# Two of four gathered groups turned by VectorE blocks and transfers inside SBUF instead of by TensorE

## The chip, the cores and the metric

The kernel runs on one core of a Trainium2 chip. The metric is the device time of one execution in microseconds (us). A kernel is run several times and the median is compared; besides, one execution is recorded by the hardware profiler, and every duration below comes from that one.

## The reference, cut to what matters

`x` is 64 batches of 32 rows by 256 features. Each batch goes through an attention block with two feed-forward nets, and then through three adapters whose weights are picked by the batch's role:

```
q, k, v = x @ Wq, x @ Wk, x @ Wv
attn_out = softmax(q k^T * scale) v @ Wp + bp
cms_out  = gelu(attn_out @ cW1 + cb1) @ cW2 + cb2 + onehot(code)
modifier = gelu(concat(attn_out, cms_out) @ mW1 + mb1) @ mW2 + mb2
x = clip(x + cms_out + modifier, 0, 1)
for layer in 3 adapters:        # weights and biases of the batch's role
    x = layernorm(x + gelu(x @ W_down + b_down) @ W_up + b_up) * gamma + beta
```

## The kernel before

Batches are sorted by role, and the 2048 rows are cut into four groups of 512 rows (`NG = 4`; the code numbers them 0 to 3, so the third and the fourth are group 2 and group 3). The feed-forward work on them runs in five waves (the last group is split in two), and the adapters of the windows (128 rows each) of one wave run in between the matmuls of the next. Everything is written out by hand, one instruction stream for each engine, with semaphores between them. A wave is a list of steps: `("H", n)` computes hidden block n on TensorE (PE), gelu and the high part of the result on ScalarE (ACT), the low part `h_lo` on VectorE (DVE); `("D", n)` multiplies that block into the result; `C` and `F` close the two nets. A matrix in float32 is split in a high and a low part and multiplied in three passes (`mm3`, lines 332 to 334).

The attention of a group is cut in parts that are hung onto such steps by the table `ATTENTION`. The rows of a group are gathered from HBM by an indirect transfer of GpSimd (POOL) into `xr`, 128 partitions of rows by 256 features, four tiles (`GT = 4`). But the matmuls want features in the partitions: `xT`. So for groups 2 and 3 part `X` (wave 0 after `H10`, wave 1 after `H5`) lets PE turn the eight 128x128 pieces into two PSUM banks (line 1365), ACT copies them to `xT` (819), ACT makes the high part `parts_hi` (822) and DVE the low part `parts_lo` (1042). Part `Y`, two steps later, multiplies them with a folded weight whose low part `fold_lo` is made by DVE (1252) just before. Then come scores `S`, softmax `P`, the weighted sum `Z` (which reads `xr` again) and the projection `A`, `B`. Groups 0 and 1 have an attention of their own at the start, in halves.

The order of the work around the change, on the two engines that issue transfers:

- POOL: gathers of groups 0 and 1; then it waits for the adapters' biases, sums two of them (`brow`, line 752); then it gathers group 2 once the `Z` of group 0 is through; and group 3 at the end of wave 0, after the `Z` of group 2, since both use the buffers of the first attention.
- SP (the sync engine's queue): weights in chunks, then some 30 transfers that pack the adapters' weights into a table in HBM (`packed_w`, `packed_rows`, lines 561 to 590; the last six, line 590, wait for DVE's `dbias`), then a wait for all of these (598, 599), then the loads of the adapters' weights window by window (606 to 614). Later layers of some windows are turned by DVE in 32x32 blocks (`block_rows`, line 1143) and moved into place by four transfers inside SBUF (`move_blocks`, line 643).

Of the kernel before, what the change touches and what calls it, by code (L numbers as in the profile page):

```python
# [12 lines left out]
P = 128  # L13
B, T, V = 64, 32, 256
H = 4 * V
# [43 lines left out]
def build(nc, x, codes, roles, Wq, Wk, Wv, Wp, bp, cW1, cb1, cW2, cb2, mW1, mb1, mW2, mb2, adapters, out):  # L59
# [3 lines left out]
    with ExitStack() as ctx:  # L63
# [3 lines left out]
        def sem(name):  # L67
            return ctx.enter_context(nc.semaphore(name))
# [175 lines left out]

        def high(cols):
            return c_hi[:, cols] if cols.stop <= MW1 else m_hi[:, cols.start - MW1:cols.stop - MW1]
# [43 lines left out]
        xT_turned = sem("xT_turned")  # L290
# [95 lines left out]
        ATTENTION = {0: {("H", 10): ("X", 2), ("H", 12): ("Y", 2), ("H", 13): ("S", 2), ("H", 14): ("P", 2),  # L386
# [147 lines left out]
        def _(sp):  # L534
# [46 lines left out]
            for layer in range(LAYERS - 1):  # L581
# [3 lines left out]
                         allow_slow_non_contiguous=True).then_inc(weights_packed, 16)  # L585
            sp.wait_ge(down_bias_ready, 1)
# [104 lines left out]
            for n, w, layer in items:  # L691
                if n and items[n - 1][1:] in moves:
                    move_blocks(*items[n - 1][1:])
                ahead = (w, layer) == (MIXED[0], 0)
                if ahead:
                    window_rows(*items[n - 1][1:])
                window_weights(w, layer)
                if 0 < n <= len(items) - len(ending) and not ahead:
                    window_rows(*items[n - 1][1:])
# [12 lines left out]
        def _(pool):  # L712
# [23 lines left out]

            def gather(g):
                for t in range(GT):
                    pool.indirect_dma_start(out=attention(g).xr[:, t, :], out_offset=None, in_=x_rows,  # L739
                                            in_offset=bass.IndirectOffsetOnAxis(ap=row_idx[:, g * GT + t:g * GT + t + 1],  # L740
                                                                                axis=0))\
                        .then_inc(x_in[g] if g >= AHEAD else half_in[2 * g + t // (GT // 2)], 16)
# [7 lines left out]
            gather(1)  # L750
            pool.wait_ge(adapter_in, 16 * ADAPTER_DMAS)
            pool.tensor_tensor(brow[:, 0, :], brow[:, 0, :], brow[:, 1, :], ALU.add).then_inc(brow_summed, 1)
            pool.wait_ge(more_consts, 3)
            pool.wait_ge(z_done, VB)
            gather(2)
# [29 lines left out]
        def _(act):  # L785
# [28 lines left out]
            def attention_part(stage_name, g):  # L814
                a = attention(g)
                if stage_name == "X":
                    act.wait_ge(xT_turned, g - AHEAD + 1)
                    for vb in range(VB):
                        act.activation(xT[:, vb, bass.ts(g, GR)], a.banks[vb][:, :], ACT.Copy).then_inc(xT_ready, 1)
                    for vb in range(VB):  # L820
                        act.wait_ge(xT_ready, 2 * VB * (g - AHEAD) + vb + 1)
                        act.activation(parts_hi[:, vb, :], xT[:, vb, bass.ts(g, GR)], ACT.Copy).then_inc(xT_ready, 1)
# [135 lines left out]
        def _(dve):  # L958
# [78 lines left out]
            def attention_part(stage_name, g):  # L1037
                a = attention(g)
                if stage_name == "X":
                    for vb in range(VB):  # L1040
                        dve.wait_ge(xT_ready, 2 * VB * (g - AHEAD) + VB + vb + 1)
                        dve.tensor_tensor(parts_lo[:, vb, :], xT[:, vb, bass.ts(g, GR)], parts_hi[:, vb, :].bitcast(F32),
                                          ALU.subtract).then_inc(xT_lo_ready, 1)
                if stage_name == "Z" and g >= AHEAD:
                    for vb in range(VB):
                        dve.wait_ge(z_ready, VB * g + vb + 1)
                        dve.tensor_tensor(parts_lo[:, vb, :], a.banks[vb][:, :], parts_hi[:, vb, :].bitcast(F32),
                                          ALU.subtract).then_inc(z_lo_ready, 1)
# [163 lines left out]
            for g, step in steps:  # L1212
# [28 lines left out]
                if g == 1 and step == ("H", 0):  # L1241
                    dve.wait_ge(eps_ready, 2 * SLOTS)
                if g == NM - 1 and step == ("H", HB + 2):
                    last_sum(last[0])
# [34 lines left out]
        def _(pe):  # L1279
# [76 lines left out]
            def attention_part(stage_name, g):  # L1356
                a, first = attention(g), g * GR
                if stage_name == "X":
                    pe.wait_ge(x_in[g], 16 * GT)
                    if g > 1:  # L1360
                        pe.wait_ge(at_hi_ready, VB * (1 if g == 2 else 3))
                        pe.wait_ge(at_lo_ready, VB * (1 if g == 2 else 3))
                    for vb in range(VB):
                        for i in range(GT):
                            ins = pe.transpose(a.banks[vb][:, i * P:(i + 1) * P], a.xr[:, i, vb * P:(vb + 1) * P],
                                               ident[:, :])
                    ins.then_inc(xT_turned, 1)
                if stage_name == "Y":
                    pe.wait_ge(xT_ready, 2 * VB * (g - AHEAD + 1))
# [20 lines left out]
                if stage_name == "Z":  # L1390
                    pe.wait_ge(pd_ready, g + 1)
                    for vb in range(VB):
                        for i in range(GT):
                            ins = pe.matmul(a.banks[vb][:, i * P:(i + 1) * P], a.xr[:, i, vb * P:(vb + 1) * P],  # L1394
                                            a.pd[:, i, :], start=True, stop=True)
                        ins.then_inc(z_done, 1)
# [327 lines left out]
```

## Time and profile before

| | |
|---|---|
| median of 3 runs | 353.15 us (353.07 to 354.5) |
| time of the profiled execution | 353.24 us |
| its span in the trace | 351.4 us |
| PE busy | 340.3 us, 97% of the span |
| DVE, ACT, POOL busy | 59%, 48%, 18% |
| granted TensorE clock | full (2.4 GHz) in every slice |
| DMA queue of SP | 33910 packets, 45.6% of 16 engines |

The span is what the trace covers; the 1.8 us between it and the time lie before the first and after the last instruction. Times "at 70.14" below are microseconds from the span's start. A matmul's own duration in the trace overlaps the next one, so what it costs is read from the distance between starts.

### The profile page before, as it was taken

To read this page: it belongs to the slowest core of one execution; us is meant where nothing else is said; L and a number is where in the kernel's file an instruction comes from. 1 tells how busy PE (TensorE), PEld (TensorE's weight loads), DVE (VectorE), ACT (ScalarE), POOL (GpSimd) and SP (SyncE) were. 2 spreads that over 40 slices of the span, in tenths; PEclk is the share of its full clock that TensorE was granted. 3 is DMA by queue.
4 is the path that set the end of the run, shared out by engine and by line. 5 is a ranking of instruction groups with operands and counts; after the bars stand their busy time and mean duration, and the time that the engine had idled before them with its cause. 6 is when DMAs were issued, how large, how long until landed. Compare 5 with 4: busy or idle time off the path is not lost.

```text
span 351.4 us, 6683 instructions
## 1 busy us (share of the span) xinstructions
PE 340.3 (97%) x2247; PEld 283.2 (81%) x2247; DVE 206.5 (59%) x493; ACT 167.3 (48%) x331; POOL 61.9 (18%) x96
## 2 busy tenths in 40 slices
PE   6899999999999999999999999999999999999994
PEld 6677687787778888788877777877899999999962
DVE  6057367350462885577464665463689777454584
ACT  3465686464543553644154455353355454634421
POOL 2710040000040110011420110013321135100221
PEclk9999999999999999999999999999999999999999
DMA  6574699558210314233176898203957432288001
GB/s 219 174 236 153 175 128 146 39 118 176 67 60 0 87 41 116 76 97 115 48 238 164 253 292 253 62 30 109 204 149 207 144 125 87 71 274 339 25 2 45
DMA packets 35704, 46.93 MB, mean 134 GB/s; under 512 B 9852, under 2 KB 20406, under 8 KB 35670
## 3 DMA queue, kind: packets, MB, share of 16 engines
q1 hardware_dynamic: 33910, 42.51, 45.6%
q0 software_dynamic: 1392, 3.80, 3.8%
q8 instruction: 18, 0.29, 0.4%
q10 hardware_dynamic: 368, 0.20, 0.2%
q14 instruction: 16, 0.13, 0.1%
HBM read 43.60 MB, written 4.48 MB: 137 GB/s over the span
## 4 chain that ended last, share of the span: by engine, by line
PE 84%; DVE 6%; ACT 3%; POOL 3%; issue 3%; DMA 1%; POOLq 0%; DVEq 0%
PE bank L332 12%; PE bank L334 11%; PE bank L333 11%; PE bank L1490 8%; PE bank L1495 8%; PE bank L1491 8%; PE bank L1537 4%; PE bank L1513 3%; PE bank L1394 2%; PE bank L1352 2%; PE bank L1412 2%; ACT h_full L847 1%; ACT h_hi L851 1%; PE bank L1568 1%; PE bank L1616 1%
## 5 line engine op out<-in xcount | busy, mean ns | idle before, releaser
L847 ACT ACTIVATE h_full<-bank,bias 128x512 f32<-128x512 f32 (+1 forms) x80 | 48.2, 603 | 111.2 <-PE bank L334 101.7
L1079 DVE TENSOR_TENSOR h_lo<-h_full,h_hi 128x512 fp32r<-128x512 f32 (+1 forms) x80 | 46.8, 585 | 60.4 <-ACT h_hi L851 57.3
L767 POOL TENSOR_TENSOR rstd<-moments,minus_half 128x1 f32<-128x1 f32 x39 | 24.9, 638 | 167.1 <-DVE moments L1152 166.9
L851 ACT ACTIVATE h_hi<-h_full 128x512 fp32r<-128x512 f32 (+1 forms) x80 | 43.7, 546 | 2.5
L1137 DVE TENSOR_TENSOR window_y<-bank,window_x 128x256 f32<-128x256 f32 x39 | 16.5, 423 | 36.9 <-PE bank L1513 25.5
L1490 PE MATMUL bank<-h_hi,m_hi 128*128 128x512 f32 (+1 forms) x80 | 30.2, 387 | 0.2
L1490 PE MATMUL bank<-h_hi,c_hi 128*128 128x512 f32 (+1 forms) x80 | 30.1, 385 | 0.2
L332 PE MATMUL bank<-at_hi,c_hi 128*128 128x512 f32 (+1 forms) x80 | 29.3, 367 | 0.0
L332 PE MATMUL bank<-at_hi,m_hi 128*128 128x512 f32 (+1 forms) x80 | 28.7, 359 | 0.0
L334 PE MATMUL bank<-at_lo,c_hi 128*128 128x512 f32 (+1 forms) x80 | 27.9, 348 | 0.0
L333 PE MATMUL bank<-at_hi,c_lo 128*128 128x512 f32 (+1 forms) x80 | 27.8, 347 | 0.0
L334 PE MATMUL bank<-at_lo,m_hi 128*128 128x512 f32 (+1 forms) x80 | 27.8, 347 | 0.0
L333 PE MATMUL bank<-at_hi,m_lo 128*128 128x512 f32 (+1 forms) x80 | 27.7, 347 | 0.0
L1491 PE MATMUL bank<-h_hi,m_lo 128*128 128x512 f32 (+1 forms) x80 | 27.2, 349 | 0.0
L1491 PE MATMUL bank<-h_hi,c_lo 128*128 128x512 f32 (+1 forms) x80 | 27.1, 348 | 0.0
L739 POOL DMA_INDIRECT xr<-in_x,row_idx x16 | 15.4, 963 | 58.8 <-PE bank L1394 49.2
L332 PE MATMUL bank<-cms_hi,m_hi 128*128 128x512 f32 (+1 forms) x70 | 24.3, 346 | 0.0
L333 PE MATMUL bank<-cms_hi,m_lo 128*128 128x512 f32 (+1 forms) x70 | 24.3, 346 | 0.0
L334 PE MATMUL bank<-cms_lo,m_hi 128*128 128x512 f32 (+1 forms) x70 | 24.2, 346 | 0.0
L1128 DVE SCALAR_TENSOR_TENSOR window_x<-window_y,rstd,adapter_rows 128x256 f32<-128x256 f32 x39 | 18.7, 480 | 5.6 <-POOL rstd L767 4.2
L1495 PE MATMUL bank<-h_lo,c_hi 128*128 128x512 f32 (+1 forms) x80 | 21.6, 351 | 0.1
L1495 PE MATMUL bank<-h_lo,m_hi 128*128 128x512 f32 (+1 forms) x80 | 21.4, 348 | 0.0
(238 smaller groups left out, 727.9 us busy)
## 6 DMA issues: line engine op xcount, KB each, us to landing
adapter_w<-packed_w SPq DMA_DIRECT2D x44, 256.5 KB, 3.6
adapter_rows<-packed_rows SPq DMA_DIRECT2D x36, 256.0 KB, 5.5
stage<-in_L_cond_mW SPq DMA_DIRECT2D x6, 512.0 KB, 5.3
mixed_w<-packed_w SPq DMA_DIRECT2D x8, 256.5 KB, 4.6
stage<-in_L_cond_cW SPq DMA_DIRECT2D x4, 512.0 KB, 6.8
last_w<-packed_w SPq DMA_DIRECT2D x2, 769.5 KB, 6.3
up_bias<-in_L_cond_b_up SPq DMA_DIRECT2D x12, 128.0 KB, 4.2
adapter_rows<-packed_rows SPq DMA_DIRECT2D x24, 64.0 KB
```

The lines of the kernel that those rows point to most:

```text
L332: pe.matmul(o, w_hi_ap, r_hi_ap, start=first, stop=False)
L333: pe.matmul(o, w_lo_ap, r_hi_ap, start=False, stop=False)
L334: return pe.matmul(o, w_hi_ap, r_lo_ap, start=False, stop=last)
L767: pool.tensor_tensor(slot.rstd[:, :], slot.moments[:, 1:2], minus_half[:, :], ALU.pow)\
L847: act.activation(h_full[:, n % 2, rows], bank[n % 2][:, rows], ACT.Gelu, bias=bias[:, b:b + 1])\
L851: act.activation(h_hi[:, n % 2, rows], h_full[:, n % 2, rows], ACT.Copy).then_inc(h_hi_ready, 1)
L1079: dve.tensor_tensor(h_lo[:, n % 2, rows], h_full[:, n % 2, rows], h_hi[:, n % 2, rows].bitcast(F32), ALU.subtract).then_inc(h_lo_ready, 1)
L1128: dve.scalar_tensor_tensor(slot.x[:, :], slot.y[:, :], slot.rstd[:, :], slot.rows[:, 1, :], ALU.mult, ALU.add).then_inc(slot.x_ready, 1)
L1137: dve.tensor_tensor(slot.y[:, :], bank[6][:, 0:V], slot.x[:, :], ALU.add).then_inc(emptied[6], 1)
L1490: pe.matmul(results[ob][:, rows], high(cols), h_hi[:, n % 2, rows], start=(j == 0), stop=False)
L1491: pe.matmul(results[ob][:, rows], low(cols), h_hi[:, n % 2, rows], start=False, stop=False)
L1495: ins = pe.matmul(results[ob][:, rows], high(cols), h_lo[:, n % 2, rows], start=False, stop=(j == HB - 1))
```

## The change

For groups 2 and 3 part `X` leaves PE. DVE transposes each row tile in 32x32 blocks (four new parts `T0` to `T3`), and SP moves each block row into `xT` by four transfers inside SBUF, 16 for a group (`spread_x`). ACT only makes the high part. Group 2's gather stands ahead of the bias sum on POOL. Group 3's `xr` is still in use when its blocks are wanted, so its rows are gathered twice: first into the columns of `xT` that group 3 will own (`x_raw`), for the blocks, and later into `xr` as before, for `Z`. The blocks of group 2 stand in `yz`, those of group 3 in the `window_y` tiles of the four adapter slots, and DVE waits before wave 1 uses these.

```diff
+        def x_blocks(g, t):
+            return (attention(g).yz[:, :, :].rearrange("p k m -> p (k m)")[:, bass.ts(t, V)] if g == AHEAD
+                    else slots[t].y[:, :])
+
+        def x_raw(t):
+            return xT[:, t // 2, bass.ds((NG - 1) * GR + t % 2 * V, V)]
...
-        ATTENTION = {0: {("H", 10): ("X", 2), ("H", 12): ("Y", 2), ("H", 13): ("S", 2), ("H", 14): ("P", 2),
+        ATTENTION = {0: {("H", 4): ("T0", 2), ("H", 5): ("T1", 2), ("H", 6): ("T2", 2), ("H", 7): ("T3", 2),
+                         ("D", 10): ("T0", 3), ("D", 11): ("T1", 3), ("D", 12): ("T2", 3), ("D", 13): ("T3", 3),
+                         ("H", 10): ("X", 2), ("H", 12): ("Y", 2), ("H", 13): ("S", 2), ("H", 14): ("P", 2),
...
+            def spread_x(g):
+
+                for t in range(GT):
+                    sp.wait_ge(x_blocked, t + 1 if g == AHEAD else 2 * GT)
+                    for q in range(Q):
+                        sp.dma_start(xT[:, :, bass.ds(g * GR + t * P + q * T, T)],
+                                     x_blocks(g, t)[quarter(q), :].rearrange("p (f m) -> p f m", f=Q)).then_inc(x_spread, 16)
+
+            spread_x(AHEAD)
             sp.wait_ge(down_bias_ready, 1)
...
+                if n == len(WAVES[1]) + 1:
+                    spread_x(AHEAD + 1)
...
+            pool.wait_ge(z_done, VB)
+            gather(2)
             pool.wait_ge(adapter_in, 16 * ADAPTER_DMAS)
             pool.tensor_tensor(brow[:, 0, :], brow[:, 0, :], brow[:, 1, :], ALU.add).then_inc(brow_summed, 1)
             pool.wait_ge(more_consts, 3)
-            pool.wait_ge(z_done, VB)
-            gather(2)
+            pool.wait_ge(down_bias_done, 1)
+            for t in range(GT):
+                gather_rows(NG - 1, t, x_raw(t))
...
                 if stage_name == "X":
-                    act.wait_ge(xT_turned, g - AHEAD + 1)
+                    act.wait_ge(x_spread, 16 * Q * GT * (g - AHEAD + 1))
                     for vb in range(VB):
-                        act.activation(xT[:, vb, bass.ts(g, GR)], a.banks[vb][:, :], ACT.Copy).then_inc(xT_ready, 1)
-                    for vb in range(VB):
-                        act.wait_ge(xT_ready, 2 * VB * (g - AHEAD) + vb + 1)
                         act.activation(parts_hi[:, vb, :], xT[:, vb, bass.ts(g, GR)], ACT.Copy).then_inc(xT_ready, 1)
...
+                if stage_name[0] == "T":
+                    t = int(stage_name[1])
+                    rows = a.xr[:, t, :] if g == AHEAD else x_raw(t)
+                    dve.wait_ge(x_in[g], 16 * GT)
+                    if g == AHEAD:
+                        dve.wait_ge(at_done, VB)
+                    dve.transpose(x_blocks(g, t).rearrange("p (f k r) -> p k f r", f=Q, k=VB),
+                                  rows.rearrange("p (k i f) -> p k f i", k=VB, f=Q)).then_inc(x_blocked, 1)
...
+                if g == 1 and step == ("H", 2):
+                    dve.wait_ge(x_spread, 16 * Q * GT * (NG - AHEAD))
...
-                if stage_name == "X":
-                    pe.wait_ge(x_in[g], 16 * GT)
...
-                    for vb in range(VB):
-                        for i in range(GT):
-                            ins = pe.transpose(a.banks[vb][:, i * P:(i + 1) * P], a.xr[:, i, vb * P:(vb + 1) * P],
-                                               ident[:, :])
-                    ins.then_inc(xT_turned, 1)
```

On PE, in wave 0 between hidden block 10 and result block 9, the rows were these before (the matmuls of the first net's output with the second net's weights, the turns, the next result block):

```order
L333 MATMUL bank<-cms_hi,m_lo 128x512
L334 MATMUL bank<-cms_lo,m_hi 128x512
L1365 MATMUL bank<-ident,xr 128x128 x8
L1490 MATMUL bank<-h_hi,m_hi 128x512
L1491 MATMUL bank<-h_hi,m_lo 128x512
```

and are these now:

```order
L341 MATMUL bank<-cms_hi,m_lo 128x512
L342 MATMUL bank<-cms_lo,m_hi 128x512
L1517 MATMUL bank<-h_hi,m_hi 128x512
L1518 MATMUL bank<-h_hi,m_lo 128x512
```

Only the eight turns are gone; the same holds in wave 1, where they stood behind the small matmuls of an adapter.

On DVE, at steps H6, H7 and C of wave 0, each chunk of weights (`m_lo`) is now followed by a transpose of one row tile of group 2 into `yz`; the last one stands between `dbias` and the sums that close the first net (`cms`):

```order
L1110 TENSOR_TENSOR h_lo<-h_full,h_hi 128x512
L1057 TENSOR_TENSOR m_lo<-stage,m_hi 128x1024
L1073 STREAM_TRANSPOSE yz<-xr 128x2x4x32
L1110 TENSOR_TENSOR h_lo<-h_full,h_hi 128x512
L1057 TENSOR_TENSOR m_lo<-stage,m_hi 128x1024
L1050 TENSOR_TENSOR dbias<-down_rows,bank 128x256
L1073 STREAM_TRANSPOSE yz<-xr 128x2x4x32
L1118 TENSOR_TENSOR cms<-bank,cms_bias 128x512 x2
```

In every one of these steps the transpose is the only row that is new, and the hidden block's low part waits behind it in the next step.

On SP, the first 16 transfers stand between the packing of `b_down` and that of `dbias`, with the loads of the adapters' weights behind them:

```order
L592 DMA packed_rows<-brow 3x256 x2
L594 DMA packed_w<-in_L_cond_b_down 384x1x1
L601 DMA xT<-yz 128x2x32 x16
L609 DMA packed_w<-dbias 128x1x1 x6
L622 TENSOR_LOAD role_table
```

The second 16 stand in the loads of wave 1, behind the weights of window 1's second layer and ahead of the rows of window 0's second layer:

```order
L625 DMA adapter_w<-packed_w 128x513
L601 DMA xT<-window_y 128x2x32 x16
L629 ISA
L629 DMA adapter_rows<-packed_rows 128x512
```

What moved is only what stands behind them in SP's own order.

## Rows read from the trace of the kernel before

**Rows 1.** The page: the chain that ended last, by engine.

```profile
PE 84%; DVE 6%; ACT 3%; POOL 3%; issue 3%; DMA 1%; POOLq 0%; DVEq 0%
```

**Rows 2.** Timeline of PE, wave 0: start us, us, engine line op out<-in.

```profile
69.91 0.39 PE L334 MATMUL bank<-cms_lo,m_hi 128*128 128x512 f32 x1
70.14 1.03 PE L1365 MATMUL bank<-ident,xr 128*128 128x128 f32 x8
70.94 0.48 PE L1490 MATMUL bank<-h_hi,m_hi 128*128 128x512 f32 x1
71.25 0.39 PE L1491 MATMUL bank<-h_hi,m_lo 128*128 128x512 f32 x1
```

**Rows 3.** The chain that ended last, its pieces at both turns: start us, us, what.

```profile
70.31 0.87 PE bank L1365 x8
...
121.39 0.87 PE bank L1365 x8
```

**Rows 4.** Timeline of PE: what DVE's work is wanted for.

```profile
63.85 0.61 PE L1453 MATMUL bank<-cms_lo,m_hi 128*128 128x512 f32 x2
...
79.29 0.47 PE L332 MATMUL bank<-parts_hi,fold_hi 128*128 128x512 f32 x1
```

**Rows 5.** Timeline of DVE, waves 0 and 1.

```profile
52.41 0.69 DVE L1079 TENSOR_TENSOR h_lo<-h_full,h_hi 128x512 fp32r<-128x512 f32 x1 [0.54 <-ACT h_hi L851]
...
59.94 0.41 DVE L1027 TENSOR_TENSOR dbias<-down_rows,bank 128x256 f32<-128x256 f32 x1
60.49 1.29 DVE L1087 TENSOR_TENSOR cms<-bank,cms_bias 128x512 f32<-128x512 f32 x2
61.88 1.29 DVE L1094 TENSOR_TENSOR cms_lo<-cms,cms_hi 128x512 fp32r<-128x512 f32 x2
...
77.93 1.22 DVE L1252 TENSOR_TENSOR fold_lo<-fold,fold_hi 128x1024 fp32r<-128x1024 f32 x1
...
94.30 1.25 DVE L1065 STREAM_TRANSPOSE pd<-expd 32x128 f32<-32x128 f32 x4
...
111.20 0.42 DVE L1163 TENSOR_TENSOR window_x<-bank,up_bias 128x256 f32<-128x256 f32 x1 [2.82 <-PE bank L1560]
...
126.31 0.63 DVE L1143 STREAM_TRANSPOSE block_rows<-window_x 128x256 f32<-128x256 f32 x1
```

**Rows 6.** Timeline of ACT around part X in wave 0.

```profile
71.60 1.07 ACT L819 ACTIVATE xT<-bank 128x512 f32<-128x512 f32 x2
72.56 1.16 ACT L822 ACTIVATE parts_hi<-xT 128x512 fp32r<-128x512 f32 x2
75.33 0.69 ACT L847 ACTIVATE h_full<-bank,bias 128x512 f32<-128x512 f32 x1 [1.62 <-PE bank L334]
```

**Rows 7.** Timeline of SP's queue: start of the issue, us it took.

```profile
51.17 1.74 SPq L578 DMA_DIRECT2D packed_rows<-in_L_cond_ln_w  x1
...
54.50 0.65 SPq L584 DMA_DIRECT2D packed_w<-in_L_cond_b_down  x1
60.38 3.76 SPq L590 DMA_DIRECT2D packed_w<-dbias  x6
...
83.24 1.49 SPq L606 DMA_DIRECT2D adapter_w<-packed_w  x1
...
126.96 2.60 SPq L643 DMA_DIRECT2D window_xT<-block_rows  x4
```

**Rows 8.** The page: issues of `move_blocks`, KB each, us to landing.

```profile
window_xT<-block_rows SPq DMA_DIRECT2D x24, 32.0 KB, 1.9
```

**Rows 9.** DMA in 139.9 to 142.6, `move_blocks` alone: packets, share of 16 engines.

```profile
DMA packets 320, 0.07 MB, mean 27 GB/s; under 512 B 320, under 2 KB 320, under 8 KB 320
...
q1 hardware_dynamic: 320, 0.07, 13.2%
```

**Rows 10.** Waits of SP's queue: us in total, times, longest.

```profile
SPq L598 <- DMA packed_rows<-brow: 4.4, 1, 4.4
```

**Rows 11.** Timeline of POOL: the first of group 2's four gathers.

```profile
43.97 0.97 POOL L739 DMA_INDIRECT xr<-in_x,row_idx  x1 [0.16 <-issue]
```

More of the change, by code:

```diff
@@ L289, in build @@
         half_y_ready = sem("half_y_ready")
-        xT_turned = sem("xT_turned")
+        x_blocked = sem("x_blocked")
+        x_spread = sem("x_spread")
         xT_ready = sem("xT_ready")
@@ L735, in _, with gather_rows @@
             pool.wait_ge(rows_known, 1)
+            def gather_rows(g, t, o):
+                pool.indirect_dma_start(out=o, out_offset=None, in_=x_rows,
+                                        in_offset=bass.IndirectOffsetOnAxis(ap=row_idx[:, g * GT + t:g * GT + t + 1], axis=0))\
+                    .then_inc(x_in[g] if g >= AHEAD else half_in[2 * g + t // (GT // 2)], 16)
             def gather(g):
                 for t in range(GT):
[L739 to L742, printed above, removed]
+                    gather_rows(g, t, attention(g).xr[:, t, :])
             def store(x_tile, w, counter):
@@ L1040, in attention_part @@
                     for vb in range(VB):
-                        dve.wait_ge(xT_ready, 2 * VB * (g - AHEAD) + VB + vb + 1)
+                        dve.wait_ge(xT_ready, VB * (g - AHEAD) + vb + 1)
                         dve.tensor_tensor(parts_lo[:, vb, :], xT[:, vb, bass.ts(g, GR)], parts_hi[:, vb, :].bitcast(F32),
                                           ALU.subtract).then_inc(xT_lo_ready, 1)
+                if stage_name[0] == "T":
[6 more added lines that the diff above has]
+                                  rows.rearrange("p (k i f) -> p k f i", k=VB, f=Q)).then_inc(x_blocked, 1)
                 if stage_name == "Z" and g >= AHEAD:
@@ L1357, in attention_part @@
                 a, first = attention(g), g * GR
-                if stage_name == "X":
-                    pe.wait_ge(x_in[g], 16 * GT)
-                    if g > 1:
-                        pe.wait_ge(at_hi_ready, VB * (1 if g == 2 else 3))
-                        pe.wait_ge(at_lo_ready, VB * (1 if g == 2 else 3))
-                    for vb in range(VB):
-                        for i in range(GT):
-                            ins = pe.transpose(a.banks[vb][:, i * P:(i + 1) * P], a.xr[:, i, vb * P:(vb + 1) * P],
-                                               ident[:, :])
-                    ins.then_inc(xT_turned, 1)
                 if stage_name == "Y":
-                    pe.wait_ge(xT_ready, 2 * VB * (g - AHEAD + 1))
+                    pe.wait_ge(at_hi_ready, VB * (1 if g == AHEAD else g))
+                    pe.wait_ge(at_lo_ready, VB * (1 if g == AHEAD else g))
+                    pe.wait_ge(xT_ready, VB * (g - AHEAD + 1))
                     pe.wait_ge(xT_lo_ready, VB * (g - AHEAD + 1))
@@ L1391, in attention_part @@
                     pe.wait_ge(pd_ready, g + 1)
+                    if g == NG - 1:
+                        pe.wait_ge(x_in[g], 16 * GT * 2)
                     for vb in range(VB):
```

## Prediction

> **What bounds the kernel now.** I read the page first: the chain that ended last is PE for 84% of the span [rows 1], at full clock everywhere, so a microsecond off PE's stream is a microsecond off the time as long as nobody makes PE wait in its place. Then the timeline of PE at the place that the edit touches [rows 2]: the matmul before the turns starts at 69.91, the turns at 70.14, the next matmul at 70.94, with no gap. Then the timelines of the engines that take over the work, DVE, ACT, SP and POOL, each for the two questions that decide the case: how long does the new work take there, and who wants its result when. PE loses no time in this stretch to DVE or ACT before the change, so every new wait would be visible at once.
>
> **What is removed.** Eight turns last from 70.14 to 70.94, 0.80 us [rows 2]. The change of kind of matmul costs on top: the first start after the turns is followed at 0.31 us (70.94 to 71.25), where 69.91 to 70.14 shows 0.23, so 0.08 more, 0.88 in all. The chain puts each set of turns at 0.87 [rows 3]. In wave 1 small float32 matmuls stand ahead of the turns, so the change of kind stays; I take 0.87 there too. Removed from the path: 0.88 + 0.87 = 1.75 us. ACT also loses its two copies of 1.07 us a group [rows 6], which are off the path.
>
> **DVE's new work.** A transpose of a 128x256 tile of this very pattern takes 0.63 us [rows 5], eight of them are 5.0 us. Seven stand in gaps. Group 2's first three come behind chunks of weights, where DVE had 0.54 idle ahead of `h_lo` [rows 5]: each overhangs by about 0.1, and PE uses the `h_lo` over a microsecond later, so nothing. The fourth stands between `dbias`, which ends at 60.35, and `cms`, which started at 60.49 [rows 5]: the transpose ends at 60.98 and all of `cms` and `cms_lo` moves by 0.49. `cms_lo` ended at 61.88 + 1.29 = 63.17 and would end at 63.66; PE wants it at 63.85 [rows 4]. The cover is 0.19, so the edit costs nothing; if each of the four did overhang by 0.1 more, PE would wait about 0.2. That is my lower and upper bound here: 0 to 0.2. Group 3's stand at D10 to D13 of wave 0, the last after the softmax blocks that end at 94.30 + 1.25 = 95.55 [rows 5]; it ends at 96.18, before PE's next need of `h_lo`.
>
> **POOL's order.** Group 2's gather started at 43.97 because it stood behind the bias sum [rows 11]; POOL sat idle ahead of that, so the gather now runs in idle time, the sum is not moved, and the rows are there long before the first transpose at about 51.9. The additional gather of group 3 starts once the down biases are computed (before `dbias` at 59.94 [rows 5]), and its user comes at about 78. Four gathers of 0.97 are issued by about 65; with the longest landing that a row here shows, some 14 us behind the packing (below, [rows 10]), they would be in at 79, a microsecond after DVE's turn and still ahead of the `h_lo` that comes next. No cost.
>
> **The transfers, group 2.** SP is free at 54.50 + 0.65 = 55.15 [rows 7]. Nothing in the trace has 128-byte runs; the nearest are those of `move_blocks`, 256-byte runs from 32 into 128 partitions: four issues in 2.60 us, 0.65 each [rows 7], 1.9 to land [rows 8]. Sixteen are 10.4 us: 55.15 + 10.4 = 65.6, the last tile's blocks (60.98) being there in time; landed at 67.5. Even if SP began only when the last tile is turned, they would land at 60.98 + 10.4 + 1.9 = 73.3. The upper bound of an issue is the 1.74 us that a small packing transfer took while SP's queue was full [rows 7]: 55.15 + 27.8 + 1.9 = 84.9. The other bound is 0.65/2 if issue went by the bytes of a run. I take 0.65: same kind of source and destination, only the runs are half as long. Who waits? ACT's part `X` started at 71.60 and the next `h_full` at 75.33 [rows 6]. The first to hurt is part `Y`: after the rows are in, ACT needs 1.16 for `parts_hi` [rows 6]; from `h_full` at 75.33 to the end of `fold_lo` at 77.93 + 1.22 = 79.15 [rows 5] are 3.82 us in one chain; together 4.98. PE reached `Y` at 79.29 [rows 4] and will reach it at 79.29 - 0.88 = 78.41. So the transfers must be in by 78.41 - 4.98 = 73.4 to cost nothing, and from 74.3 on the first 0.88 are used up. By my value the cover is 73.4 - 67.5 = 5.9 us.
>
> **How much the DMA engines have to do.** Alone, `move_blocks` shows 320 packets in 2.7 us at 13.2% of 16 engines [rows 9]: 0.132 x 16 x 2.7 / 320 = 17.8 ns a packet. A group's transfers are 16 x (256 + 16) = 4352 packets, 272 an engine: 4.8 us by that price, 2.4 if half the bytes are half the time. Either is below the 10.4 of the issue, so SP's issue decides, not the engines. The weights' packing moves behind it: the six `dbias` transfers from 60.38 [rows 7] to 65.6, and the adapters' loads by 5 us. These loads ended at 83.24 + 1.49 = 84.7 [rows 7] and the first window's sum comes at 111.2 [rows 5]: no cost.
>
> **A rule that speaks against it.** The `packed_rows` of the bias sum were issued before 54.50, and SP still waited 4.4 us for them [rows 10] after its last issue at 60.38 + 3.76 = 64.14 [rows 7], so they counted as landed at 68.5, some 14 us after the issue, where a move inside SBUF took 1.9 [rows 8]. The Trainium skill says why in "DMA: Bandwidth & Descriptors", Queues, rings and completion order: a transfer's completion count is written only after every earlier write of the same DMA engine. By that rule, the trace agrees as far as that row goes. As a mechanism of this kernel, from the rows alone: the new transfers stand behind those slow packing writes, so they would count at 68.5, plus their own 4.8 us of engine time, plus 1.9 to land: 75.2, which is 1.8 too late for `Y`. By the free landing (67.5) the sum is -1.75, by this one -1.75 + 1.8 = 0. I hold the free landing for likelier, since group 2's gather no longer runs among the packing [rows 11] and the backlog should end earlier; the other is a rival.
>
> **The transfers, group 3.** They wait for all eight transposes, 96.18 - 0.88 = 95.3, are issued by 105.7 and landed by 107.6. SP has nothing else to do then: its loads are out, and the next waits for window 0. DVE waits for them before wave 1 touches `window_y`, after the row at 111.20 + 0.42 [rows 5], now 110.7. Cover 3.1 us; an issue of more than (110.7 - 95.3 - 1.9)/16 = 0.84 us uses it up.
>
> **Sum.** 353.24 - 1.75 + 0 = 351.5 for the profiled execution, which stands 0.1 above the median: 351.4 for the median. A change of 0.5% (1.77 us) is about what can be told from none, so this gain is right at that edge.
>
> **Rivals.**
> - *The turned rows of group 2 come late*: packing and moves share the queues, and completion waits for the slow writes. For it the wait of 4.4 us [rows 10] and the issue of 1.74 [rows 7]. Against it that the backlog ends earlier without the gather. At the landing of 75.2 it costs 1.8: 353.2; at the bound of 84.9 it would cost 11.5: 362.9. Chance 0.13.
> - *Group 3's transfers stall DVE* (the one on the other side): if 128-byte runs cost more to issue. At 1.1 us each they land at 95.3 + 17.6 + 1.9 = 114.8, DVE is 4.1 late, and if PE follows the time is 351.4 + 4.1 = 355.5; it is slower than before from an issue of (110.7 + 1.75 - 95.3 - 1.9)/16 = 0.95 us, and by over 0.5% from 1.06. For it: twice the runs of `move_blocks`. Against it: each of these was 0.65 whatever else went on. Chance 0.08.
> - *Part of the gain is given back in small waits*: the overhangs on DVE with only 0.19 of cover at `cms`, `fold_lo` ending 0.14 ahead of `Y`, later waits that do not move with PE. Half of the gain: 352.3. Chance 0.17.
>
> **How the numbers follow.** The forecast, all of the gain, has 0.62. Its own spread is small, 350.8 to 351.8, and it lies on the edge of 0.5%, so I split it. Faster by over 0.5%: 0.62 x 0.65 = 0.40, the larger share because ACT's lighter load may add some tenths. Same: 0.62 x 0.35 = 0.22, with 0.17 and the 0.09 of the first rival that stay near 353.2: 0.48. Slower by over 0.5%: the other 0.04 of it and 0.08, 0.12. The range runs from 350.8 to 354.6, which takes in a small wait and a landing up to 3 us late.
>
> **What would show it.** Right: no rows of turns, 0.23 between the matmuls there; the 16 issues near 0.65 each, ACT's `parts_hi` at about 71 with no wait behind a DMA; PE's `Y` near 78.4; DVE's wait at 110.7 not visible. Wrong: an ACT wait named by a DMA into `xT`, `Y` after 79.3, DVE idle ahead of the first `window_y`, SP issues above 0.84 us, or idle time of PE ahead of the matmuls at 63.85.

## The result and the profile after

The changed kernel takes 357.6 us (median of 6 runs, 356.66 to 358.25), the kernel before took 353.56 us beside it (6 runs, 353.05 to 354.5). The ratio is 1.0113, 95% interval 1.01 to 1.0126: slower, outside my range. The profiled execution took 357.25 us, its span is 355.4, 4.0 more than before. Of the kernel before's executions beside e1 to e3, the three with a mean granted clock of 0.992 took 354.2 to 354.4 us, the ten others 353.0 to 353.4.

The page of the changed kernel, the chain that ended last by engine, where [rows 1] stood before.

```profile
PE 81%; DVE 7%; ACT 3%; POOL 3%; issue 3%; another core or an unknown queue 2%; DMA 1%; POOLq 0%; DVEq 0%
```

PE has gone from 84% to 81%, and 2% of the chain stand behind something that the profile can't name. That share is one single piece. The chain in order of time:

```profile
26.25 2.36 DVE c_lo L1057 x2
28.61 6.03 another core or an unknown queue
...
34.66 0.30 DVE row_max L1084
```

`row_max` is the first step of group 1's softmax, ahead of wave 0: nothing of this is near the turns. The timeline of POOL shows what is new at 28.6, the early gather of group 2:

```profile
28.75 0.95 POOL L759 DMA_INDIRECT xr<-in_x,row_idx  x1 [9.98 <-PE bank L1421]
30.00 0.94 POOL L759 DMA_INDIRECT xr<-in_x,row_idx  x1 [0.30 <-issue]
...
32.50 0.95 POOL L759 DMA_INDIRECT xr<-in_x,row_idx  x1 [0.30 <-issue]
```

The timeline of PE in the kernel before, at group 1's scores (64 matmuls of 32 columns), the projection, and, behind Z, the first matmul of wave 0:

```profile
27.48 0.76 PE L1387 MATMUL bank<-xT,yz 128*32 128x32 f32 x64
28.18 3.70 PE L1412 MATMUL bank<-yz,fold 128*128 128x512 f32 x8
...
33.65 0.47 PE L332 MATMUL bank<-at_hi,c_hi 128*128 128x512 f32 x1
```

The same of the changed kernel, up to wave 0's first matmul at 39.63:

```profile
28.41 0.60 PE L1412 MATMUL bank<-xT,yz 128*32 128x32 f32 x45
29.32 0.27 PE L1412 MATMUL bank<-xT,yz 128*32 128x32 f32 x6 [0.31 <-issue]
30.07 0.28 PE L1412 MATMUL bank<-xT,yz 128*32 128x32 f32 x6 [0.48 <-issue]
30.83 0.28 PE L1412 MATMUL bank<-xT,yz 128*32 128x32 f32 x5 [0.48 <-issue]
31.59 0.24 PE L1412 MATMUL bank<-xT,yz 128*32 128x32 f32 x2 [0.48 <-issue]
31.76 5.40 PE L1439 MATMUL bank<-yz,fold 128*128 128x512 f32 x8
37.82 2.05 PE L1421 MATMUL bank<-pd,xr 128*128 128x128 f32 x16 [0.66 <-DVE pd L1096]
39.63 0.48 PE L340 MATMUL bank<-at_hi,c_hi 128*128 128x512 f32 x1
```

Read it from the top. The two traces are already 0.93 us apart when the scores start (28.41 and 27.48), and this is not the change's doing (e2 below, the same code up to there, starts them at 27.56). The windows (us of the stretch, then the busy share with the number of instructions for PE, PEld, DVE, ACT and POOL, then granted clock, DMA share, GB/s) show it at 16, first in the changed kernel, then in the one before:

```profile
16.00:17.00 1.00, 1.00 (x5) 0.91 (x4) 0.00 (x0) 0.37 (x1) 0.69 (x2) 0.50 0.36 110
```

```profile
16.00:17.00 1.00, 1.00 (x8) 0.90 (x7) 0.00 (x0) 0.70 (x2) 0.69 (x2) 1.00 0.31 73
```

The changed kernel's trace has the granted clock at 0.50, the 1.2 GHz level, from 15 to 19, after three microseconds with PE busy for 0.07, 0.49 and 0.68 (0.82, 0.66 and 0.39 in the kernel before, where it stayed full). The traces of e7 and e11 below have the same fall and start their first scores about a microsecond late; no other has it.

In the changed kernel PE gets through 45 of the 64 matmuls, and then pauses after every five or six, with nothing named that it waits for. The scores take 3.4 us and not 0.76. The first pause comes some 0.25 us after the first gather's issue began. The gathered rows' own packets start only after 31, behind the first three pauses. Then the projection takes 5.40 us for the same eight matmuls. The windows of that stretch show why:

```profile
28.00:29.00 1.00, 1.00 (x50) 0.79 (x49) 0.61 (x1) 0.70 (x2) 0.25 (x1) 1.00 0.52 119
29.00:30.00 1.00, 0.28 (x7) 0.16 (x5) 0.00 (x0) 0.11 (x1) 0.70 (x1) 1.00 0.97 333
30.00:31.00 1.00, 0.44 (x11) 0.34 (x11) 0.00 (x0) 0.00 (x0) 0.94 (x1) 1.00 0.83 259
31.00:32.00 1.00, 0.52 (x8) 0.38 (x4) 0.00 (x0) 0.00 (x0) 0.75 (x1) 1.00 1.00 328
32.00:33.00 1.00, 1.00 (x3) 0.26 (x3) 0.00 (x0) 0.00 (x0) 0.69 (x2) 0.73 0.73 256
33.00:34.00 1.00, 1.00 (x3) 0.48 (x2) 0.00 (x0) 0.00 (x0) 0.45 (x1) 0.50 0.45 160
```

PE was busy for 0.28, 0.44 and 0.52 of three microseconds, and then the granted clock fell to 0.50; it was back at 1.00 in 36 to 37. In all, the first matmul of wave 0 starts at 39.63 where it started at 33.65, 5.98 late. Of this 0.93 stood before the scores. The other 5.05 is the burst (from the start of the scores to that of the projection 3.35 and not 0.70: 2.65), the projection at the lower clock (5.40 and not 3.70: 1.70), and 0.66 that PE then waits for DVE's `pd`, because `row_max` came late; some 0.04 is rest. Since PE ends up waiting for `pd`, it is the late `row_max` (34.66) that sets the time there: at full clock PE would only have waited longer. The end is only 4.0 late, so 1.98 came back on the way: the gain that I had forecast is there, below a loss that I had not seen.

### The profile page after: what moved, and what is told of

Read it like the earlier page. It is cut to its first block, busy times and chain, and to the rows that moved or that the text cites. A ratio compares the mean times of both kernels' runs of the same rounds, so it can differ in the third digit from the quotient of the medians.

```text
span 355.4 us, 6696 instructions
## 1 busy us (share of the span) xinstructions
PE 341.7 (96%) x2231; PEld 283.3 (80%) x2231; DVE 210.5 (59%) x501; ACT 165.5 (47%) x327; POOL 65.6 (18%) x100
## 4 chain that ended last, share of the span: by engine, by line
PE 81%; DVE 7%; ACT 3%; POOL 3%; issue 3%; another core or an unknown queue 2%; DMA 1%; POOLq 0%; DVEq 0%
PE bank L340 12%; PE bank L342 12%; PE bank L341 11%; PE bank L1517 9%; PE bank L1522 8%; PE bank L1518 8%; PE bank L1564 4%; PE bank L1540 3%; PE bank L1421 2%; PE bank L1385 1%; DVE pd L1096 1%; PE bank L1595 1%; PE bank L1643 1%; ACT h_full L870 1%
## 5 line engine op out<-in xcount | busy, mean ns | idle before, releaser
L793 POOL TENSOR_TENSOR rstd<-moments,minus_half 128x1 f32<-128x1 f32 x39 | 24.0, 616 | 166.8 <-DVE moments L1183 166.7
```

What stands on the lines that cost most here:

```text
L793: pool.tensor_tensor(slot.rstd[:, :], slot.moments[:, 1:2], minus_half[:, :], ALU.pow)\
```

## The experiments

Each row of the table was timed against the kernel before in alternating runs on one chip. The rounds ran on three chips (kernel before: 353.26 us beside e1 to e3, 352.71 beside e4 to e7, 353.35 beside e8 to e10, 353.05 beside e11 to e14), so compare rows of different rounds by their ratios. "Early" means the moment of the changed kernel: when group 0's Z products are done and PE turns to group 1's scores.

| run | made of | time, us | ratio (95%) |
|---|---|---|---|
| e1_before_early | before, four gathers early | 358.38 | 1.0145 (1.0118 to 1.0171) |
| e2_after_later | changed, gathers after both Z | 351.66 | 0.9959 (0.9944 to 0.9975) |
| e3_after_behind_sum | changed, gathers behind the bias sum | 363.86 | 1.0285 (1.0247 to 1.0322) |
| e4_before_after_scores | before, four gathers just after the scores | 352.71 | 1.0012 (0.999 to 1.0035) |
| e5_before_one_early | before, one gather early | 352.8 | 1.0006 (0.9989 to 1.0023) |
| e6_before_pool_busy | before, POOL computing early | 352.63 | 0.9997 (0.9978 to 1.0016) |
| e7_before_act_rows | before, plain transfers by ACT early | 352.98 | 1.001 (0.9985 to 1.0034) |
| e8_after_scores | changed, gathers just after the scores | 352.59 | 0.999 (0.9965 to 1.0015) |
| e9_before_pool_plain | before, plain transfers by POOL early | 353.41 | 1.0005 (0.9991 to 1.0018) |
| e10_before_two_early | before, two gathers early | 357.52 | 1.01 (1.0075 to 1.0125) |
| e11_before_first_scores | before, four more gathers at group 0's scores | 357.5 | 1.0115 (1.0096 to 1.0134) |
| e14_before_gather_then_plain | before, a gather and three plain early | 354.77 | 1.0048 (1.0032 to 1.0063) |
| e12_after_later_again | as e2 | 351.32 | 0.9946 (0.9929 to 0.9962) |
| e13_after_scores_again | as e8 | 351.3 | 0.9946 (0.9928 to 0.9963) |

**First round: is it the early gather, and nothing else?** e1 takes the kernel before and makes that edit alone:

```diff
+            pool.wait_ge(z_done, VB)
+            gather(2)
             pool.wait_ge(adapter_in, 16 * ADAPTER_DMAS)
...
-            pool.wait_ge(z_done, VB)
-            gather(2)
```

> The kernel before with one edit: group 2's gather on GpSimd stands ahead of the bias sum, right after the weighted sum of group 0. Theory A (the early gather itself starves TensorE while it computes the scores of group 1, and its clock then falls): the scores at 28 us show gaps, the next matmuls run at half clock, wave 0 starts some 6 us late, time about 359. Theory B (the stall comes from something else in the change, such as the new transfers, waits or where the code lies): no gaps, time 353.5.

358.38 us, more than the changed kernel itself, since nothing is gained here. The timeline of its PE shows the same pauses:

```profile
27.48 0.60 PE L1387 MATMUL bank<-xT,yz 128*32 128x32 f32 x45
28.39 0.28 PE L1387 MATMUL bank<-xT,yz 128*32 128x32 f32 x5 [0.31 <-issue]
...
30.90 5.08 PE L1412 MATMUL bank<-yz,fold 128*128 128x512 f32 x8
```

Wave 0 starts 5.09 late, by the same sum: 2.72 in the burst, 1.38 in the projection, 0.96 of waiting for `pd`. One of its other executions, with a mean clock of 1.00, took 358.4 us too, which fits: with four gathers the low clock costs nothing on top. So the loss is made by the gather's new place alone; this kernel still has the turns on PE and none of the new transposes and transfers. e2 takes the changed kernel and lets POOL wait for the Z products of both groups:

```diff
             gather(1)
-            pool.wait_ge(z_done, VB)
+            pool.wait_ge(z_done, 2 * VB)
             gather(2)
```

> The changed kernel with one edit: group 2's gather waits for the weighted sum of group 1 (z_done 4 in place of 2), so it is issued at about 34 us, still ahead of the bias sum and well ahead of its first transpose at 52. Theory A: no gaps at the scores, start as before, both sets of turns gone: 351.7. Theory B: 357.6 as the changed kernel.

351.66 us: faster than both kernels, and on my forecast of 351.4 within its scatter. Its gathers run from 34.01, in wave 0. PE has no pause at the scores, and reaches part `Y` where the prediction had it:

```profile
27.56 0.76 PE L1412 MATMUL bank<-xT,yz 128*32 128x32 f32 x64
...
33.72 0.47 PE L340 MATMUL bank<-at_hi,c_hi 128*128 128x512 f32 x1
...
78.40 0.47 PE L340 MATMUL bank<-parts_hi,fold_hi 128*128 128x512 f32 x1
```

e3 puts the gather back to where it stood before, behind the bias sum:

```diff
-            pool.wait_ge(z_done, VB)
-            gather(2)
             pool.wait_ge(adapter_in, 16 * ADAPTER_DMAS)
...
             pool.wait_ge(down_bias_done, 1)
+            pool.wait_ge(z_done, VB)
+            gather(2)
```

> The changed kernel with group 2's gather back behind the bias sum, where it stood before (issued from 44 us on). Theory A: the start is as before, but the rows land among the packing at about 63, so the first transpose waits from 52 on and VectorE holds up the low parts behind it: a wait of some 10 us in wave 0, time about 358 to 362 with the stall in another place. Theory B: gaps at the scores as in the changed kernel and that wait on top, above 362.

363.86 us, the slowest of all, with a start as in the kernel before. The waits of its DVE name the cause:

```profile
DVE yz L1073 <- DMA xr<-in_x,row_idx: 12.2, 1, 12.2
```

While PE stood still behind that wait, the clock fell to 0.50 (from 60 to 68). The four gathers were issued from 44.26 on and their rows counted as landed 12.2 us after DVE wanted them for its first transposes, so an earlier gather is part of what the change needs. It has a window: after the scores, well ahead of 51.8.

**Second round: what in the early gather does it?** Four edits of the kernel before, each with one suspect. e4 adds one wait to e1, `pool.wait_ge(scores_done, 2)` ahead of the gather.

> The kernel before with group 2's gather ahead of the bias sum, but waiting for the scores of group 1 as well, so it is issued from about 28.4 us on, some 0.7 us later than in the first experiment. Theory A1 (the harm needs the burst of 64 tiny score matmuls to coincide with the gather's issue on GpSimd): no gaps, time 353.3. Theory A2 (the issue of a gather slows TensorE or the semaphores between 28 and 33 us whatever it runs, for instance through the load on the DMA engines): the projection matmuls behind the scores run slow or show gaps, time 356 to 359.

352.71 us, no loss: the gathers started at 28.23, 0.78 after the scores' end at 27.45, and ran until 32.9 beside the projection and Z, which took 3.70 and 1.95 as ever. Gathers that meet these larger matmuls cost nothing. e5 gathers one tile early and three after both Z:

```diff
+            pool.wait_ge(z_done, VB)
+            gather(2, range(1))
+            pool.wait_ge(z_done, 2 * VB)
+            gather(2, range(1, GT))
```

> The kernel before with one of the four gathers of group 2 right after the weighted sum of group 0 (some 27.8 us), the other three after that of group 1 (34 us). Theory A1 with a cost by the length of the collision: gaps for about 1.2 us, then the scores run on; time 354.5 to 355. If any gather at that point triggers the whole stall: 358.4. If only the queue of several gathers does it: 353.3.

352.8 us. Its gather ran from 27.22 to 28.16, right over the scores, and these took 0.92 instead of 0.76:

```profile
26.88 0.92 PE L1389 MATMUL bank<-xT,yz 128*32 128x32 f32 x64
27.87 3.69 PE L1414 MATMUL bank<-yz,fold 128*128 128x512 f32 x8
```

Read by the distance between starts (0.99 from the scores to the projection, 0.70 before), one gather costs PE 0.29 us, which is too little to tell in the time. e6 has POOL compute instead (eight powers on 128x15 values, 22 us in all, into columns of `xT` that are overwritten later):

```diff
+            pool.wait_ge(z_done, VB)
+            for n in range(8):
+                pool.tensor_tensor(xT[:, 0, 3 * GR + n * 15:3 * GR + (n + 1) * 15],
+                                   ident[:, 0:15], ident[:, 0:15], ALU.pow)
```

> The kernel before, its gather where it was, with eight power operations of 128x15 elements on GpSimd in the place where the early gathers stood (they write columns that are overwritten later). Rival to the gather (any work of GpSimd in that stretch starves the others, through the SBUF port or otherwise): stall as in the first experiment, about 358. Theory A: no stall, 353.3.

352.63 us, scores in 0.76: a busy POOL is not the cause. e7 has ACT's queue send four plain 128-row transfers into `xr` (the real gather overwrites them later):

```diff
+            for t in range(GT):
+                act.dma_start(first_attention.xr[:, t, :], x_rows[t * P:(t + 1) * P, :]).then_inc(early_rows, 16)
```

> The kernel before with four plain transfers of 128 rows each from HBM into the buffer of group 2's rows, issued by ScalarE's queue at about 28.3 us; the real gather stays behind the bias sum. The same bytes at the same time without GpSimd's descriptors. If the bytes on the DMA engines do the harm: stall, about 358. If it is the issue on GpSimd: 353.3 to 354.5 (ScalarE's issues cost it 1.5 us, of which it had 0.75 idle).

352.98 us, no gap. ACT issued them from 28.66 to 30.5 and the scores ran from 28.54 to 29.30, so the issue met them and most of the bytes did not. That bytes are not what holds PE back rests rather on the changed kernel, where the first three pauses came before the gather had moved any.

**Third round: how many, and of which kind.** e9 moves e7's four plain transfers to POOL's own queue, at the early moment (`pool.dma_start` after `pool.wait_ge(z_done, VB)`).

> The kernel before, with four plain transfers of 128 rows (no list of rows) issued by GpSimd at the moment where the early gather stood; the real gather stays behind the bias sum and overwrites them. If it is the making of any descriptors on GpSimd that holds back the score matmuls: gaps between the small matmuls as with the early gather, a first wave up to 5 us later, 356 to 358.5. If it is the gather by a list of rows alone: no gaps, 353.

353.41 us. POOL issued all four in 2.24 us, from 27.87 on, over scores that started at 27.50 and took 0.76. So the same engine, the same moment and the same number of transfers do no harm when they are plain. e10 is e5 with `range(2)` early.

> The kernel before, with two of the third group's four tiles gathered at the early moment and two after both Z products. If every gather issue that meets the scores holds them back for as long as it lasts: gaps of some 0.5 us until the second gather has been issued, about 30.3, the softmax's first step some 2.5 us late instead of 5.5, 354.5 to 356. If only the whole row of four does harm (a queue that fills): 353.

357.52 us. Two gathers do it:

```profile
27.55 0.60 PE L1389 MATMUL bank<-xT,yz 128*32 128x32 f32 x45
28.47 0.28 PE L1389 MATMUL bank<-xT,yz 128*32 128x32 f32 x5 [0.32 <-issue]
...
30.71 0.32 PE L1389 MATMUL bank<-xT,yz 128*32 128x32 f32 x3 [0.49 <-issue]
30.96 5.08 PE L1414 MATMUL bank<-yz,fold 128*128 128x512 f32 x8
```

My own picture, a pause that lasts as long as a gather is being issued, doesn't fit: POOL had issued the second by 30.10, and pauses came until 30.7, as long as with four. The share of the effects can be read here. `row_max` started at 31.07, 2.78 later than before [28.29], but the first matmul of wave 0 at 37.81, 4.16 later: the projection's longer time at the lower clock (5.08 against 3.70) was on the path too. With two gathers `row_max` follows the scores at once, and the sum is 2.71 in the burst and 1.38 in the projection, 4.09 from the start of the scores. The three other timed executions took 356.0, 357.65 and 357.71 us; the one of 356.0 had a mean granted clock of 1.00, the others and the traced one 0.994 to 0.995, which fits a price of about 1.4 for the low clock.

**Fourth round: only at that place? And which later place is best?** e11 leaves the kernel before as it is and adds four gathers (the third group's rows, into `xT` columns that are overwritten later) where group 0's scores may start:

```diff
+            pool.wait_ge(half_y_ready, 2)
+            for t in range(GT):
+                pool.indirect_dma_start(out=xT[:, t // 2, 3 * GR + t % 2 * V:3 * GR + (t % 2 + 1) * V], ...)
+            pool.wait_ge(early_rows, 16 * GT)
```

> The kernel before, with four more gathers (the third group's rows, into columns of xT that are overwritten later) issued when the first group's scores can start, at about 20.9. If any row of two or more gathers that meets a burst of the 64 small matmuls holds it back: gaps of 0.5 to 0.7 us after every 5 or 6 matmuls of the first group's scores, a start that shifts by 2.5 to 3 us where the burst's end is waited for, and perhaps a lower clock. If it is something of the second group's place alone: no gaps at 21, 353.

357.5 us, 1.0115. The traced execution was by far the mildest of the five (354.47, the others 357.4 to 358.8), and shows one pause of 0.18 behind the 46th matmul:

```profile
22.05 0.61 PE L1394 MATMUL bank<-xT,yz 128*32 128x32 f32 x46 [0.25 <-ACT yz L818]
22.85 0.38 PE L1394 MATMUL bank<-xT,yz 128*32 128x32 f32 x18 [0.18 <-issue]
```

(It starts a microsecond late by the early fall of the clock, which makes up most of the 354.47.) So gathers near group 0's scores cost about 4 us as well, and make a pause there; that the other four executions lost their time in such pauses is likely, not shown. e14 queues three plain transfers behind one gather:

```diff
+            gather(2, range(1))
+            for t in range(1, GT):
+                pool.dma_start(attention(2).xr[:, t, :], x_rows[t * P:(t + 1) * P, :]).then_inc(early_rows, 16)
```

> The kernel before, with one gather and three plain transfers in a row behind it on GpSimd at the early moment (the three real gathers stay behind the bias sum). One gather alone and four plain transfers alone did no harm; two gathers did. If it is a second gather by a list of rows that does it: one gap of 0.15 us at most, 353. If it is anything queued behind a gather: gaps of 0.5 to 0.7 us, a first wave 4 us later, 357.

354.77 us, between the two forecasts. The traced execution took 354.2:

```profile
27.46 0.60 PE L1393 MATMUL bank<-xT,yz 128*32 128x32 f32 x45
28.36 0.28 PE L1393 MATMUL bank<-xT,yz 128*32 128x32 f32 x5 [0.30 <-issue]
29.07 0.36 PE L1393 MATMUL bank<-xT,yz 128*32 128x32 f32 x14 [0.44 <-issue]
29.36 3.70 PE L1418 MATMUL bank<-yz,fold 128*128 128x512 f32 x8
```

Two pauses, then the rest of the burst at full pace, and in this execution no fall of the clock. Five of the ten took 354.0 to 354.3 us, the other five 355.3 to 355.7 at a mean clock of 0.995; whether the clock fell behind the burst in those, no trace shows. So it is dosed by what stands behind the first gather: from the start of the scores to that of the projection (0.70 before) it takes 0.29 more with nothing behind it, 1.2 more with plain transfers, 2.7 more with a second gather.

The versions with the early moment given up: e8 adds the wait for `scores_done` to the changed kernel.

```diff
             pool.wait_ge(z_done, VB)
+            pool.wait_ge(scores_done, 2)
             gather(2)
```

> The changed kernel, with its third group's gather held back until the second group's scores are done (some 1.5 us later than in the changed kernel, some 4 us earlier than in the version that waited for both groups' Z products). If the loss comes only from gather issues that meet the 64 small score matmuls: the first wave starts at about 33.7, no gap in the scores, 351.7 within 0.5, and nothing further is gained over the version with the later gather, since nobody waits for these rows before 51. If an early gather costs the changed kernel something by itself: 353 or more.

352.59 us, with a scatter from 351.6 to 356.17 and an interval of the ratio that takes in 1. The scores had no pause, but part `Y` was late. ACT, PE and SP of its trace:

```profile
75.22 1.16 ACT L846 ACTIVATE parts_hi<-xT 128x512 fp32r<-128x512 f32 x2 [3.23 <-DMA xT<-yz]
...
80.22 0.47 PE L340 MATMUL bank<-parts_hi,fold_hi 128*128 128x512 f32 x1 [1.47 <-DVE fold_lo L1286]
...
55.79 18.01 SPq L601 DMA_DIRECT2D xT<-yz  x16
```

I ran both later versions again on one chip.

> The changed kernel with the third group's gather after both Z products once more, beside the version after the scores on the same chip. If the two differ by where the transfers inside SBUF land (72.3 in the one, 75.2 in the other, with 73.4 as the point from which the wave waits) and that differs from run to run: both between 351.2 and 353, medians within 0.6. If the place of the gather itself matters: this one at 351.7, the other at 352.6.

> The changed kernel with the third group's gather after the second group's scores once more, on the same chip as the version after both Z products. If the landing of the sixteen transfers varies from run to run: a median within 0.6 us of the other's. If the earlier gather is the worse place: 352.6 against 351.7.

351.32 and 351.3 us: the same. On this chip the place of the gather, once it is past the scores, doesn't matter. In e13's trace the rows were in at 71.82 and PE didn't wait, where e8, the same kernel on another chip, had them at 75.22. SP was free of the packing 1.9 later there, and the sixteen issues took 18.0 and not 15.5; why is open.

## Why the prediction was wrong, point by point

**The step that failed** is "POOL's order": "POOL sat idle ahead of that, so the gather now runs in idle time, the sum is not moved, and the rows are there long before the first transpose", and "No cost". Each half is true for POOL: it was idle, and the rows were in time. What I never asked is what PE does at that moment. It was the one burst of tiny matmuls in the neighbourhood, 64 in 0.76 us, and two or more gathers queued over it cost 4.1 us (e10) to 5.1 us (e1, and the changed kernel), before any of the turned rows is used. The term stood at 0, and it measured 5.05. Of my rivals none had this mechanism, and my range ended at 354.6, so it had no room for it.

**What is removed** was right. In e2 PE reached `Y` at 78.40, where I had 78.41 from [rows 4]: 79.29 less 0.88. The span ended at 349.6 against 351.4, 1.8 less, with 1.75 forecast. In the changed kernel the same shows as 5.98 late at wave 0 and 4.0 late at the end.

**DVE's new work** was right. Its transposes took 0.62 to 0.64. The fourth pushed `cms` by some 0.3, where I had computed 0.49, and the cover at PE held: in the changed kernel the row that stood at 63.85 [rows 4] has no wait.

```profile
66.25 0.62 DVE L1073 STREAM_TRANSPOSE yz<-xr 128x256 f32<-128x256 f32 x1
66.80 1.24 DVE L1118 TENSOR_TENSOR cms<-bank,cms_bias 128x512 f32<-128x512 f32 x2
68.15 1.29 DVE L1125 TENSOR_TENSOR cms_lo<-cms,cms_hi 128x512 fp32r<-128x512 f32 x2
```

```profile
69.82 0.62 PE L1480 MATMUL bank<-cms_lo,m_hi 128*128 128x512 f32 x2
```

**The transfers, group 2**: the mechanism was right, a term was mis-sized. I took 0.65 us an issue from [rows 7], the `move_blocks` of a later stretch. Here the transfers stand right behind the packing of the weights. SP and ACT of the changed kernel:

```profile
59.69 15.34 SPq L601 DMA_DIRECT2D xT<-yz  x16
```

```profile
78.09 1.16 ACT L845 ACTIVATE parts_hi<-xT 128x512 fp32r<-128x512 f32 x2 [0.42 <-DMA xT<-yz]
```

That is 0.96 each on the mean. Of e2, where the start is undisturbed (the last line is L601 alone: shortest, median and longest issue in ns):

```profile
54.23 16.67 SPq L601 DMA_DIRECT2D xT<-yz  x16
...
95.42 10.59 SPq L601 DMA_DIRECT2D xT<-window_y  x16
...
72.32 1.16 ACT L845 ACTIVATE parts_hi<-xT 128x512 fp32r<-128x512 f32 x2 [0.61 <-DMA xT<-yz]
...
L601 SPq DMA_DIRECT2D xT<-yz x16: 610/616/2661, 54.2 to 69.8; - x16
```

1.04 each on the mean for group 2, 0.66 for group 3. The mean hides two kinds: the median is 0.62, near the forecast, and the excess is in the first six issues (up to 2.66) and the last (1.12). So the 128-byte runs cost nothing more than the 256-byte ones; the first issues were held up. That the packing still in SP's queue does it fits [rows 7] (1.74 for a small one), and no run tests it. Landed at 72.3, not 67.5: of 5.9 us of cover 1.1 were left (to 73.4). e8 shows both the threshold and the price behind it: SP was free 1.6 later, the rows landed at 75.2, and PE waited 1.47. So my first rival was near, and its number (75.2) came true in e8 by another way. For it I had cited the Trainium skill, "DMA: Bandwidth & Descriptors", Queues, rings and completion order, with a landing of 75.2 worked out from rows. The traces don't decide for that rule: in e2 and e8 ACT went on 1.42 us after SP's last issue (70.90 to 72.32, 73.80 to 75.22), less than the 1.9 of [rows 8], so there the delay was in the issues. In the changed kernel it was 3.06 (75.03 to 78.09), and in e13 2.43 (69.39 to 71.82); whether completions waited for older writes there is open.

**The transfers, group 3** were right: 0.66 an issue. In the changed kernel the last was issued at 111.96, and DVE's first `window_y` has a wait for PE ahead of it and none for a DMA:

```profile
118.11 0.42 DVE L1168 TENSOR_TENSOR window_y<-bank,window_x 128x256 f32<-128x256 f32 x1 [1.39 <-PE bank L1540]
```

**Part of the gain given back** in small waits did not happen in e2: PE reached `Y` within 0.01 of the forecast. The 1.47 of e8 is the first rival's wait, not this one's.

## What to carry to other kernels

"The engine is idle there" is only half of an argument for moving an issue: look at what every other engine does at the new moment, and above all whether TensorE runs a burst of tiny matmuls, whose loss can be paid twice when the clock falls behind it (e10). Move gathers by a list of rows past such a burst with one wait (here on `scores_done`): that turned a loss of 4.0 us (ratio 1.0113) into a gain of 1.75 in e13 (0.9946), and into nothing clear of noise in e8 (0.999). And size the issue of transfers by rows of the same queue in the same stretch, and by single issues, not by their mean: here the same transfer took 0.61 us in most issues and up to 2.7 right behind the packing.

## What the runs showed that I had not expected

- Two or more indirect gathers in a row on GpSimd, begun 0.35 us into a burst of 64 matmuls of 32 columns, made TensorE pause 0.3 to 0.5 us after every 5 or 6 matmuls. One gather cost 0.29 us, POOL's arithmetic nothing, four plain transfers from POOL nothing, plain transfers behind one gather 1.2 us. The pauses began behind matmul 45 or 46. The projection (512 columns) and `Z` (128 columns) beside the same gathers kept their pace.
- What TensorE waited for stays open: the profile names nothing ("issue"). That it is the small size of the matmuls that makes them vulnerable is inferred from e4; no run changed their size. SP's load of weights was in flight over group 1's scores as well (DMA share 0.76 in the kernel before from 27.5 to 28.3), so whether gathers would do this with idle DMA engines is untested too.
- With four gathers, `row_max` started 2.8 us after the last score matmul in the trace, and about 1.2 us after POOL had ended its last issue (33.45 and 34.66 in the changed kernel, 32.51 and 33.77 in e1); with two it started at once. Why DVE was released so late is open.
- After three microseconds with PE busy for 0.28 to 0.52 of the time the granted clock fell to the 1.2 GHz level for about three, which added 1.4 to 1.7 us to eight matmuls. With two gathers that was on the path, with four it was hidden under the wait for `row_max`.
